# Where VectorE takes the reciprocal of the softmax sums in a neighbourhood-attention layer

## The reference

```
xn = layernorm(x); q, k, v = split(xn @ w_qkv + b_qkv)
attn = softmax(q . k(7x7 window) * scale + rpb)          # per token and head, 49 neighbours
out  = sum over the window of attn * v
x = x + out @ w_proj + b_proj
x = x + gelu(layernorm(x) @ w_fc1 + b_fc1) @ w_fc2 + b_fc2
t = layernorm(x); t = t + (t @ Wq + bq) * sum_tokens((t @ Wk + bk) * (t @ Wv + bv))
t = t + spectral_filter(layernorm(t))                    # the second half of the kernel
```

## Time and profile before

| what | us |
|---|---|
| time, median of 3 runs | 1770.49 (1768.07 to 1772.65) |
| the profiled execution, its time | 1771.29 |
| its span in the trace | 1770.0 |
| PE busy | 1652.3 (93%) |
| DVE busy | 1320.9 (75%) |
| ACT busy | 1219.7 (69%) |
| POOL busy | 743.7 (42%) |

### The profile page before, as it was taken

How to read it: one execution, slowest core, us unless ns; L and a number is a source line. 1 busy time by engine, 2 the same in 40 slices (tenths; PEclk the granted TensorE clock), 3 DMA queues, 4 the chain that set the end, 5 groups by cost and what they waited for, 6 DMA issues and landing times.

```text
span 1770.0 us, 76295 instructions
## 1 busy us (share of the span) xinstructions
PE 1652.3 (93%) x32219; PEld 1346.7 (76%) x32219; DVE 1320.9 (75%) x3860; ACT 1219.7 (69%) x2712; POOL 743.7 (42%) x979
## 2 busy tenths in 40 slices
PE   5899999998999998897899999999999999999997
PEld 3577776666676766797788888888888888888674
DVE  2677788888876876687567777777777777776886
ACT  5788888887877755555767777777777677775232
POOL 6555555655554554121324443434453345531011
PEclk8899999999999998898999999999999999999998
DMA  4432333333332322377613333343233333335874
GB/s 119 118 85 77 98 94 83 89 103 98 90 100 77 98 73 54 103 224 249 204 37 85 72 79 67 65 90 84 65 76 74 71 85 76 75 69 148 199 148 73
DMA packets 278979, 175.90 MB, mean 99 GB/s; under 512 B 92082, under 2 KB 272480, under 8 KB 277042
## 3 DMA queue, kind: packets, MB, share of 16 engines
q1 hardware_dynamic: 263968, 151.00, 30.7%
q0 software_dynamic: 12288, 19.63, 7.8%
q10 hardware_dynamic: 2384, 0.40, 0.2%
HBM read 100.41 MB, written 83.46 MB: 104 GB/s over the span
## 4 chain that ended last, share of the span: by engine, by line
PE 67%; DVE 14%; issue 5%; POOL 5%; ACT 5%; DMA 2%; SPq 1%; DVEq 0%; POOLq 0%; ACTq 0%
PE banks L1410 21%; PE banks L1388 11%; PE banks L1391 10%; PE banks L413 6%; DVE zone L619 4%; PE banks L1709 3%; PE banks L1696 3%; PE banks L407 2%; DVE st L606 2%; PE banks L372 2%; DVE W L661 1%; ACT zone L563 1%; PE banks L420 1%; PE banks L362 1%; PE banks L460 1%
## 5 line engine op out<-in xcount | busy, mean ns | idle before, releaser
L1450 DVE COPY Gm<-banks 128x448 f32<-128x448 f32 x896 | 549.2, 637 | 183.0 <-PE banks L1388 108.8
L1429 ACT ACTIVATE Gm<-banks 128x448 f32<-128x448 f32 x896 | 515.9, 625 | 212.7 <-PE banks L1388 154.7
L1410 PE MATMUL banks<-Gm,U 128*32 128x128 f32 x12544 | 513.7, 274 | 8.4 <-POOL U L1505 6.9
L1410 PEld LDWEIGHTS banks<-Gm,U 128*32 128x32 f32 x12544 | 336.3, 110 | 50.6 <-issue 43.6
L1391 PE MATMUL banks<-V,zone 118*32 118x224 bf16 x7040 | 292.8, 259 | 3.3 <-issue 3.3
L881 POOL TENSOR_TENSOR W<-W,mx 128x280 f32<-128x280 f32 x196 | 130.2, 664 | 222.7 <-DVE mx L668 222.3
L1388 PE MATMUL banks<-V,zone 118*128 118x224 bf16 x1824 | 215.9, 261 | 1.3 <-ACT qT L1215 0.5
L1525 POOL DMA_DIRECT2D Yd<-Zd x102 | 78.8, 773 | 297.6 <-DMA Yd<-Zd 273.0
L1391 PEld LDWEIGHTS banks<-V,zone 118*32 118x32 bf16 x7040 | 192.6, 96 | 5.1 <-issue 4.1
L1388 PEld LDWEIGHTS banks<-V,zone 118*128 118x128 bf16 x1824 | 156.0, 98 | 49.6 <-issue 39.5
L527 ACT ACTIVATE W<-W,mx 128x140 f32<-128x140 f32 x392 | 156.2, 402 | 0.3
(11 more groups left out here) (193 smaller groups left out, 2654.0 us busy)
## 6 DMA issues: line engine op xcount, KB each, us to landing
W<-Vd SPq DMA_DIRECT2D x392, 49.0 KB
Yd<-YS SPq DMA_DIRECT2D x28, 448.0 KB, 4.8
Zd<-YS SPq DMA_DIRECT2D x56, 224.0 KB, 3.3
UL<-Ud SPq DMA_DIRECT2D x27, 448.0 KB, 4.5
Yd<-Zd POOLq DMA_DIRECT2D x95, 112.0 KB, 3.3
YL<-Yd SPq DMA_DIRECT2D x40, 196.0 KB
zone<-Mbf SPq DMA_DIRECT2D x28, 256.0 KB
Vd<-W SPq DMA_DIRECT2D x56, 112.0 KB
```

Of the source, the lines that this page charges most:

```text
L1410: ins = e.matmul(p[32 * x:32 * x + 32, :], self.U7[(2 * P + ch) % 3][:, sl, 8 * (3 - q):8 * (3 - q) + 32], self.Gm[:, par, r:r + 2, :], st ...
L1429: e.activation(dst, src, ACT.Copy).then_inc(S["gm_act"], 1)
L1450: v.tensor_copy(dst, src).then_inc(S["gm_dve"], 1)
```

## The change

In every step the item inv stood first, and it was that of the tile three steps back. Now it stands behind smax of the step, and is that of the tile two steps back: the same reciprocal, issued on DVE earlier in the list by whatever lay between the smax of one step and the beginning of the next. No instruction is added, removed or altered, and no semaphore.

```
@@ order_ab @@
         kept = [x for x in kept if x not in done]
-        order += tile((3, "inv")) + kept + ([] if paired else row) + first.get(u, [])
+        order += kept + ([] if paired else row) + first.get(u, [])
         order += tile((4, "turn"), (3, "snorm"), (2, "prob"))
...
         cut = next((i + 1 for i, (k, _) in enumerate(parts) if k in MIDDLE), 0)
-        order += parts[:cut] + tile((0, "smax")) + parts[cut:] + fill.get(u, [])
+        order += parts[:cut] + tile((0, "smax"), (2, "inv")) + parts[cut:] + fill.get(u, [])
```

## The result

The change makes the kernel slower: 1784.3 us (median of 6 runs, 1781.1 to 1786.5) against 1771.1 us (6 runs of the kernel before, 1765.7 to 1772.8). The ratio is 1.0078, interval 1.0060 to 1.0096, that is 11 to 17 us. The forecast was 1770.1 us, the range ended at 1778: wrong, in size and in sign.

A forecast was written before the change was run, and what follows sets the result against it. PE was taken to lead the chain from 100 to 245 and 500 to 690 us, DVE between. Terms -1.85 + 2.0 - 0.5 = -0.35 us gave 1770.9 us, 1770.1 as a median; range 1761 to 1778.

The forecast's parts named there:

- PE's waits for snorm: Turn on PE, 100 to 245 us: waits for snorm fall from 3.0 us to about 1.4.
- tile 30: Turn on PE near 119 us: snorm comes earlier, but keep limits the gain to 0.35 of 0.81 us.
- tile 35: Turn on PE at 137.42 us: its 0.20 us wait for snorm goes whole.
- the second effect: DVE: the earlier reciprocal may wait for prob and hold work behind it; idle time before m_add2 covers this, counted 0.
- exchange of equals: DVE beside snorm: for most tiles one instruction is slowed as another is freed, no net cost.
- one step (93): Snorm of tile 91 slows m_norm22 by 0.34 us and no longer slows u_norm4, by the same 0.34 us.
- the third effect: Snorm runs beside other DVE instructions; 245 to 500 us: +2.0 us in four rows, -0.5 us in the others.
- 1.85 us: PE up to 245 us: shorter waits for snorm, 1.05 plus 0.80 us, passed on whole; bounds 0 and 3.2 us.
- step 102: Near 350 us, where L890, snorm and L908 meet: +0.5 us, or -0.5 us if L908 does not hold L830.
- signs of being wrong: First layer: reciprocal waits for prob before other work than m_add2; PE's 100 to 245 us shortens over 3 us or not.
- (b): 245 to 500 us: back-to-back POOL instructions keep DVE out, 1.0 us later per row; 1778.6 us, chance 0.18.
- (a): DVE relieved: L908 and L890 catch fewer norms, one less in each of 9 rows; 1760 us, chance 0.24.

The follow-up runs named there:

- x12: Reciprocal early only in the 34 steps with mixing and no norm behind smax, elsewhere as in the kernel before; 1767.8 us, ratio 0.9999 to the kernel before.
- x3: Two reciprocals per tile: the first waits for prob at the new place, a second releases snorm at the old; 1776.5 us, ratio 1.0041 to the kernel before.
- x4: Control of x3: both reciprocals per tile at the old place; 1772.8 us, ratio 1.0028 to the kernel before.
- x5: Reciprocal at the new place but of the neighbouring tile's sums, POOL's snorm waiting for prob itself; 1780.3 us, ratio 1.0059 to the kernel before.
- x6: Control of x5: the neighbour's reciprocal at the old place, snorm waiting for prob itself; 1768.9 us, ratio 0.9995 to the kernel before.
- x2: Reciprocal early only in steps where norms, mixing or other port work follows smax, otherwise at the old place; 1778.5 us, ratio 1.0048 to the kernel before.
- x1: Reciprocal early only in steps where nothing but moments follows smax, otherwise at the old place; 1770.3 us, ratio 1.0006 to the kernel before.
- x8: Changed kernel, reciprocal at the new place, with snorm cut to 70 of 280 columns; 1757.9 us, against 1757.4 us with the reciprocal at the old place.
- x11: Reciprocal later than in the kernel before: behind u_norm, just ahead of smax, where a step begins with one; 1763.8 us, ratio 0.9977 to the kernel before.
- y1: Reciprocal early only in some 50 steps with m_norm and no c_norm behind smax; 1777.3 us, ratio 1.0042 to the kernel before.
- y2: Reciprocal later than in the kernel before: behind any norm a step begins with, ahead of smax; 1771.7 us, ratio 1.0011 to the kernel before.

## Why the prediction was wrong

**Right.** PE's waits for snorm. For tile 30 the prediction says that keep bounds the gain and 0.35 of 0.81 us go. In x12, where little else moves, PE's turn is:

```profile
122.36 0.62 PE L374 MATMUL banks<-ident,W 128*98 128x128 f32 x4 [0.46 <-ACT W L539]
```

0.46 us are left and the wait is for keep, which is what was forecast from the earlier trace rows. In the kernel after it is 0.26 us, and the wait of tile 35 is gone. From 100 to 245 us no wait for snorm is left (forecast about 1.4 us). Nearly right is the second effect: L668's idle time for ACT grows from 38.9 to 52.2 us (13.3, forecast 6 to 12) and m_add2's for PE falls from 42.8 to 25.0 us; x3 against x4 prices the wait at about 2.3 us, not zero, and x5 against x6 shows that the loss does without it.

**The step that failed: "For most tiles this is an exchange of equals."** It was read off one step (93), where the hold moves from u_norm to m_norm, and the price of the third effect was then looked for only where L890, snorm and L908 meet, from 245 to 500 us. The count says otherwise: 54 more DVE instructions are held, for 20 us. Up to 245 us there is no u_norm yet, so a hold of m_norm is exchanged for nothing: 20 more are held, 7.8 us, where the sum had nothing but the gain of 1.85 us. From 500 to 720 us, where the sum had 0, 18 more are held, 10.1 us. Eight times a p_sum (L740) that ran free now lasts 0.33 us longer, at the p_sum in front of which the reciprocal went; 18 more instructions run into the inverse root L843; and three pairs like that of step 95 are caught by three POOL instructions in a row. Both lists say why: where norms or mixing end a step, the old order issued them ahead of the reciprocal, so that snorm began when they were through; the new one releases snorm right in front of them. x2 and x1 show this as the place of the loss, x8 that it takes a long snorm. That held time turns into lost time by way of smax and PE's wait for it is read from the traces of the steps above; no experiment takes that link alone.

**The step worked out in full went the other way.** For step 102 I took +0.5 us and kept -0.5 as the lower end. The kernel after:

```profile
356.30 0.15 DVE L668 RECIPROCAL mx<-mx 128x2 f32<-128x2 f32 x1
356.37 1.55 DVE L619 TENSOR_SCALAR zone<-XR,zone 112x128 f32<-112x128 f32 x2
357.84 0.34 DVE L828 TENSOR_SCALAR zone<-zone,wsel 128x256 f32<-128x256 f32 x1
358.29 0.69 DVE L830 SCALAR_TENSOR_TENSOR zone<-zone,wsel 128x256 f32<-128x256 f32 x1
358.90 0.68 DVE L649 TENSOR_TENSOR W<-banks,zone 112x512 f32<-112x512 f32 x1
359.50 0.95 DVE L619 TENSOR_SCALAR zone<-XR,zone 112x128 f32<-112x128 f32 x2
...
356.57 1.26 POOL L890 TENSOR_TENSOR XR<-XR,zone 112x512 f32<-112x512 f32 x1
357.80 0.89 POOL L881 TENSOR_TENSOR W<-W,mx 128x280 f32<-128x280 f32 x1
358.65 1.45 POOL L908 TENSOR_TENSOR XR<-XR,zone 112x512 f32<-112x512 f32 x1
```

L828 went through beside snorm and made it 0.89 us long; L830 got in ahead of L908, which was itself slowed to 1.45 us. From the first pair to the end of the second it is 359.50 + 0.95 - 356.37 = 4.08 us; before, 352.10 + 1.55 - 349.11 = 4.54 us. So the gain of 0.46 us that I kept as a bound came, and the loss of the layer came mostly from steps that I had priced at nothing or less.

**"I let the 1.85 us pass."** They did not. DVE's later norms and smax took their place on PE at once: fc2 of row 1 is already 0.9 us late, that of row 7 2.5 us, where 1.85 us less was forecast. Two of the prediction's own signs of being wrong are met with that: PE's time from 100 to 245 us did not shorten, and a reciprocal waits for prob in front of other work than m_add2 (26 of 35 waits in the first layer, 7 of 29 before). The row period from fc2 of row 7 to that of row 17 (241 to 486 us) grew by 0.45 us, where 0.3 was allowed.

**The rivals.** (b) came nearest in time (1778.6) and in the engine it named. Its mechanism, a waiting DVE instruction that misses a boundary between two POOL instructions, exists, as step 95 shows. But misses did not become more frequent: where an L619 waits at such a boundary, it gets in 23 times and misses 10 times before, 37 and 5 times after (counted: copies over 0.40 us long that run across the end of a POOL instruction with the next less than 0.05 us behind). What grew is how often the two engines meet, and three of the misses are longer than any before, 1.4 us against at most 1.17. Of (a), fewer catches, the stretch from 245 to 500 us had a part: the copies L619 lose 3.5 us of holding there, and other instructions take it up (L830, L740). With a later release more came, in x11.

The Trainium skill, "SBUF — State Buffer", section "Who interferes with whom", has this contention as an exclusive lock of the port pair, held for a whole instruction by whoever starts first. The traces agree: 172 of the 192 held L619 of both kernels end 0.08 to 0.09 us behind the POOL instruction in their way (333.09 and 333.01 in step 95), and x8 takes the loss away by shortening that instruction. The prediction cited the rule, and then applied it to one kind of step only.

**What stays open.** How much of the loss is the clock's: the six runs of the kernel after have a mean granted clock of 0.972 to 0.976, 103 runs of the kernel before in the experiments a median of 0.980. x5 loses 11.4 us to x6 at nearly the same clock (0.978 and 0.979), so the move costs most of it without; whether PE's longer waits bring the drops about, the runs do not show. The lost time by fc2 of row 27 is 9.6 us, the median loss 13.2 us. The rest arises in the spectral part, whose code is equal; there profiled executions differ by themselves (x4 is at +0.9 us at row 27 and at +10.6 us at the end), so whether the change has a part in these 4 us isn't settled. Nor is what decides whether a waiting L619 gets in at a boundary. And why x12's 7 us of holding cost nothing, while y1's 12 us cost 7, was argued only: m_add2's idle time may absorb some.

## What to carry to other kernels

Before a producer's release is moved, list what will run beside the released instruction at its new time, not only who waits for it: here 9 us fewer waits for snorm on PE came with 20 us more of held DVE instructions and 13 us more of the kernel. Count such meetings over all steps of a period and in every stretch, not in the one step that looks worst. The sum of held time is not the price, though: x12 holds 7 us more for nothing, and step 95 gives back 0.9 of the 1.5 us by which its pair is longer. Where two engines share ports, a release can be worth delaying until the port work in front of it is issued: x11 gained 4 us that way, and y2 shows that the consumer's wait sets the limit.

## What the runs showed of the hardware

A waiting DVE instruction does not surely get in when one POOL instruction ends and the next is ready: one L619 lasted 1.40 us through L890's rest and all of snorm. The contention goes both ways in the same stretch: with L828 beside it snorm took 0.89 us instead of 0.65, and L908 behind L830 1.45 us instead of 1.28. An instruction with two inputs in SBUF is caught like the tensor_scalar copies: L740 from 425 to 754 ns in all 8 cases, L719 from 284 up to 1358 ns. A wait of PE of 1.8 to 2.0 us was followed by 3.4 us at the lower clock in five of ten cases between 245 and 500 us; the waits of 1.12 us at these places in the kernel before were not.
